# Causal masks of pass one written into PSUM by the scalar engine instead of by matmuls, the slots of both passes put side by side, and one sum moved to GpSimd

## The reference, cut to what matters

```python
x  = L0_attn_x                                   # (32, 256, 128): 32 images of 256 tokens
xn = layernorm(x)
# branch 1: rotary attention, 16 heads of width 8
scores = einsum(q_rot, k_rot) / sqrt(8) + decay_bias      # (b, 16, 256, 256)
scores = where(causal, scores, -inf)
attn_1 = softmax(scores) @ v ;  out_1 = attn_1 @ Wo.T
# branch 2: one head of width 128 whose q, k, v, o are mixtures over 8 experts,
# gated by rw = gating(layernorm(xn)); then a gated mixture of 8 experts as feed-forward
hs    = n + attn_out ;  out_2 = hs + moe(layernorm(hs))
return x + out_1 + out_2
```

## Time and profile before

| what | value |
|---|---|
| median of 3 runs | 1262.35 us (1260.88 to 1263.69) |
| the profiled execution, its own time | 1263.52 us |
| its span, first to last instruction | 1261.7 us |
| granted TensorE clock, mean (1 is full speed) | 0.985 |
| PE busy | 1177.7 us, 93% |
| DVE busy | 1030.4 us, 82% |
| ACT busy | 710.2 us, 56% |
| POOL busy | 220.9 us, 18% |
| start of the first mask product (L1498) of step 1, of step 30 | 98.58 us, 951.33 us |

### The profile page before, as it was taken

The page is one execution under the profiler, slowest core; times in us unless marked ns, Lnnn a source line. Parts: engine busy times, 40 slices in busy tenths (PEclk is TensorE's granted clock), DMA queues, the critical chain, the costliest instruction groups (busy, mean ns, idle before and its releaser), DMA issues.

```text
span 1261.7 us, 33146 instructions
## 1 busy us (share of the span) xinstructions
PE 1177.7 (93%) x10652; PEld 899.4 (71%) x10652; DVE 1030.4 (82%) x3704; ACT 710.2 (56%) x1286; POOL 220.9 (18%) x338
## 2 busy tenths in 40 slices
PE   2399999999999999999999999999999899999998
PEld 1167777777777777777777777777777677777776
DVE  8878888888888888888888888888876667777664
ACT  2155565665666666655666666666665744555532
POOL 4212222222222222222222222222223000000000
PEclk9789999999999999999999999999999999999999
DMA  3433332333333333323323333333331044444453
GB/s 97 131 109 91 89 91 85 89 100 95 111 85 91 88 88 87 90 87 95 85 85 88 96 107 101 88 87 91 90 85 55 10 157 169 169 170 179 188 188 132
DMA packets 103113, 133.01 MB, mean 105 GB/s; under 512 B 13576, under 2 KB 82424, under 8 KB 94864
## 3 DMA queue, kind: packets, MB, share of 16 engines
q1 hardware_dynamic: 100548, 130.72, 33.3%
q10 hardware_dynamic: 2508, 1.58, 0.4%
HBM read 109.12 MB, written 21.54 MB: 104 GB/s over the span
## 4 chain that ended last, share of the span: by engine, by line
PE 45%; DVE 29%; issue 15%; ACT 7%; DVEq 3%; DMA 1%; POOL 0%; ACTq 0%; SPq 0%; POOLq 0%
PE ps L1838 9%; PE ps L1824 9%; PE ps L1621 4%; DVE mx L1175 3%; PE ps L1448 3%; PE ps L1552 3%; ACT ps L759 3%; ACT pr L753 3%; PE ps L1575 2%; PE ps L1576 2%; DVE rots L1100 2%; PE ps L1611 2%; DVE rots L1091 2%; PE ps L1585 1%; DVE rots L1095 1%
## 5 line engine op out<-in xcount | busy, mean ns | idle before, releaser
L753 ACT ACTIVATE pr<-ps 128x1024 f32<-128x1024 f32 x192 | 196.7, 1025 | 109.4 <-PE ps L1535 76.2
L1175 DVE TENSOR_REDUCE mx<-ps 128x4 f32<-128x1024 f32 (+1 forms) x192 | 234.9, 1224 | 20.1 <-PE ps L1508 12.0
L621 POOL TENSOR_TENSOR n1s<-rep,n1T 128x256 f32<-128x256 f32 x256 | 177.0, 729 | 299.5 <-DVE mpart L1189 279.5
L759 ACT ACTIVATE ps<-trn 128x1024 f32<-128x1024 bf16 x191 | 196.4, 1028 | 4.1
L1838 PEld LDWEIGHTS ps<-w2s,ats 128*128 128x128 f32 x1024 | 131.7, 192 | 51.2 <-issue 46.8
L1575 PE MATMUL ps<-n1s,wqk 128*128 128x256 f32 x512 | 163.7, 402 | 0.0
L1576 PE MATMUL ps<-n1s,wqk 128*128 128x256 f32 x512 | 153.2, 381 | 0.0
L950 ACT ACTIVATE n1s<-ps 128x512 f32<-128x512 f32 x128 | 76.5, 597 | 123.1 <-PE ps L1824 121.9
L1585 PE MATMUL ps<-wv,n1s 128*128 128x128 f32 x1024 | 141.6, 281 | 0.0
L1838 PE MATMUL ps<-w2s,ats 128*128 128x128 f32 x1024 | 135.7, 276 | 1.9 <-DVE ats L1378 1.9
L1585 PEld LDWEIGHTS ps<-wv,n1s 128*128 128x128 f32 x1024 | 126.7, 191 | 11.5 <-issue 6.5
(11 more groups left out here) (230 smaller groups left out, 2041.0 us busy)
## 6 DMA issues: line engine op xcount, KB each, us to landing
rep<-scr_rw SPq DMA_DIRECT2D x32, 1024.0 KB, 5.7
stk<-scr_rw SPq DMA_DIRECT2D x16, 1024.0 KB, 8.0
scr_parts<-parts SPq DMA_DIRECT2D x64, 192.0 KB, 5.8
stk<-scr_parts SPq DMA_DIRECT2D x248, 48.0 KB
rots<-scr_rw SPq DMA_DIRECT2D x8, 1024.0 KB, 4.7
wqk<-scr_rw SPq DMA_DIRECT2D x8, 1024.0 KB, 9.3
stk<-scr_parts SPq DMA_DIRECT2D x248, 32.0 KB
xt<-in_x SPq DMA_DIRECT2D x32, 128.0 KB, 2.1
```

What stands on the lines that cost most here:

```text
L621: pool.tensor_tensor(n1s[:, e], rep[:, par, e], n1T[:, par], ALU.mult).then_inc(n1s_done, 1)
L753: act.activation(pr[:, Q, :, i], ps[:, S2[0]:S2[0] + NF], ACT.Exp).then_inc(exp_done, 1)
L759: act.activation(ps[:, S2[0]:S2[0] + NF], seeds[:, kind:kind + 1].broadcast_to((P, NF, 512)), ACT.Copy).then_inc(seed_done, 1)
L1175: dve.tensor_reduce(mx[:, min(i, 1)].rearrange("p (f h) -> p f h", f=NF)[:, :, h:h + n], ps[:, S1[0]:S1[0] + NF].rearrange("p f (h t) -> p ...
```

## The change

Four things are done.

1. `mask_l`, `mask_r`, `mask_half`, their eight DMAs, three VectorE instructions and all mask products of `unit1` are gone. A new tile `seeds1` (two kinds, bf16) is made in the prologue, and ScalarE's new `seed_max(b, k)` copies it over both banks of S1 before each unit of pass one. It waits until `row_max` of the unit before has read them; `unit1` waits for `seed1_done`.
2. ScalarE's and TensorE's orders are rearranged: on TensorE unit2(k) stands right behind unit1(k) everywhere, and qk 0 goes ahead of unit1(0); on ScalarE seed_max(n + 1, k + 1) stands right behind exps(n, k), and that of unit 0 at the end of the step before.
3. The sum `bs` moves from VectorE's add_hs to GpSimd's new `add_base`, the last thing in GpSimd's step.
4. In the prologue GpSimd's scale(0) no longer waits for max_parts(0). The transposes of norm_T and the products of proj set their start flag on the first one of a bank only; the banks of S1 are prepared by `plant_seeds` too.

```diff
+            def seed_max(b, k, front=None):
+                act.wait_ge(s1_read, UNITS * b + k)
+                if front is not None:
+                    act.wait_ge(rot_chain, ROT_LINKS * front + 2)
+                kind = 1 if k % 3 else 0
+                act.activation(ps[:, S1[0]:S1[0] + NF], seeds1[:, kind:kind + 1].broadcast_to((P, NF, 512)), ACT.Copy
+                               ).then_inc(seed1_done, 1)
...
 ScalarE, step:
                 exps(n, 0)
+                next_seed(1)
...
                 exps(n, 1)
+                next_seed(2)
...
                 exps(n, 2)
+                next_seed(3)
...
+                exps(n, 3)
                 evac_qk(n)
-                exp_slot(n, 3)
+                next_seed(4)
                 evac_pv(n, 0)
-                seed_slot(n, 3)
+                exps(n, 4)
+                next_seed(5)
...
                 soft_exp(n)
-                exps(n, 4)
...
                 if n_x:
                     put_max(n + 1, 1 - u)
+                if n_x >= 2:
+                    seed_max(n + 2, 0, n + 3 if n_x == 3 else None)
...
 ScalarE, prologue:
+            seed_max(0, 1)
             evac_weights(0)
             evac_logits(1)
             evac_v(1, 1)
+            for k in range(2, 4):
+                seed_max(0, k)
             upper_stacks(1, 1, 0, stack_in)
+            seed_max(0, 4)
+            seed_max(0, 5)
             gate_tanh(1)
             upper_stacks(1, 1, 1, stack_in)
...
             evac_norm_x(2, LATER)
+            seed_max(1, 0, 2)
...
 TensorE, unit1:
-                pe.wait_ge(s1_read, UNITS * b + k)
-                for f in range(NF):
-                    bank = ps[:, S1[f]]
-                    if i == 0:
-                        mm(bank, mask_l[ROWS[f]], mask_r[ROWS[f]].rearrange("p h t -> p (h t)"), start=True, stop=False,
-                           skip_group_check=True)
-                    else:
-                        mm(bank.rearrange("p (h t) -> p h t", h=2)[:, :, P:S], mask_l[ROWS[f]], mask_r[ROWS[f], 0:2],
-                           start=True, stop=False, skip_group_check=True)
+                pe.wait_ge(seed1_done, UNITS * b + k + 1)
...
 TensorE, step:
+                qk(n, 0)
                 next_max(0)
                 unit2(n, u, 0)
-                qk(n, 0)
                 qk(n, 1)
...
                 next_max(3)
+                unit2(n, u, 3)
                 qk(n, 7)
-                unit2(n, u, 3)
                 pv(n, u, 0)
...
                 next_max(4)
+                unit2(n, u, 4)
                 soft_scores(n)
                 ve(n, 0)
                 out_T(n, 0)
                 ve(n, 1)
                 ve(n, 2)
+                ve(n, 3)
                 next_max(5)
-                unit2(n, u, 4)
+                unit2(n, u, 5)
...
-                for e in range(3, 7):
+                for e in range(4, E):
                     ve(n, e)
-                unit2(n, u, 5)
-                ve(n, 7)
...
 GpSimd:
-                pool.wait_ge(max_chain, (MAX_LINKS + 1) * (b + 1))
+                if not isinstance(b, int) or b:
+                    pool.wait_ge(max_chain, (MAX_LINKS + 1) * (b + 1))
...
+            def add_base(n, u):
+                pool.wait_ge(hs_done, n + 1)
+                pool.wait_ge(xa_done, n + 1)
+                pool.wait_ge(base_stored, 16 * n)
+                hv = hs[:, T * n:T * n + T] if isinstance(n, int) else hs[:, bass.ds(n * T, T)]
+                pool.tensor_tensor(bs[:, u], hv, xa[:, u], ALU.add).then_inc(base_done, 1)
...
 VectorE, add_hs:
-                dve.wait_ge(hs_done, n + 1)
-                dve.wait_ge(xa_done, n + 1)
-                dve.wait_ge(base_stored, 16 * n)
-                dve.tensor_tensor(bs[:, u], hv, xa[:, u], ALU.add).then_inc(base_done, 1)
```

More of the change, by code:

```diff
@@ L49 @@
 STACK_DMAS = NF * (1 + SLOT_DMAS)
-NEAR, FAR, FAINT = 2.0 ** 41, 2.0 ** 126, 2.0 ** -85
 LN2_LINKS = 3 + 10
@@ L94 @@
 BIAS_LINKS = 9
-CASTS = 5
+CASTS = 8
 BF16_ONES = float(np.array([0x3F803F80], np.uint32).view(np.float32)[0])
@@ L146, in build @@
         mask_in = sb("mask_in", [P, 2, P])
-        mask_half = sb("mask_half", [P, 4, P])
         mask_qk = sb("mask_qk", [P, 2, P], BF16)
-        mask_l = sb("mask_l", [P, P], BF16)
-        mask_r = sb("mask_r", [P, HG, P], BF16)
+        seeds1 = sb("seeds1", [P, 2, 512], BF16)
         wa = sb("wa", [P, 5, D])
@@ L248, in build @@
         FIRST, LATER = (G0, PVB), (S1[0], S1[1])
-        ld_const, ld_w, ld_half, cb_stored = sem("ld_const"), sem("ld_w"), sem("ld_half"), sem("cb_stored")
+        ld_const, ld_w, cb_stored = sem("ld_const"), sem("ld_w"), sem("cb_stored")
         ld_ident, ld_theta, ld_sim, ld_wa, ld_w2, rows_in = (
             sem("ld_ident"), sem("ld_theta"), sem("ld_sim"), sem("ld_wa"), sem("ld_w2"), sem("rows_in"))
-        sim_chain, bias_chain, mask_made, cast_done = (
-            sem("sim_chain"), sem("bias_chain"), sem("mask_made"), sem("cast_done"))
+        sim_chain, bias_chain, cast_done = sem("sim_chain"), sem("bias_chain"), sem("cast_done")
         set_dve, set_act, set_pe, set_pool, set_dma = (
@@ L296, in build @@
         seed_done = sem("seed_done")
+        seed1_done = sem("seed1_done")
         exp_done = sem("exp_done")
@@ L638, in step @@
                     scale(n + 1, 1 - u)
+                add_base(n, u)
             second_norm(0)
@@ L685, in make_seeds @@
                 act.activation(seeds[:, 1].rearrange("p (h t) -> p h t", h=HG), mask_in[:, 1:2].broadcast_to((P, HG, P)),
+                               ACT.Copy).then_inc(cast_done, 1)
+                halves = seeds1[:, 1].rearrange("p (h a t) -> p h a t", h=2, a=2)
+                act.activation(halves[:, :, 0], ones_p[:].rearrange("p (o t) -> p o t", o=1).broadcast_to((P, 2, P)),
+                               ACT.Copy, scale=0.0).then_inc(cast_done, 1)
+                act.activation(halves[:, :, 1], mask_in[:, 0:1].broadcast_to((P, 2, P)), ACT.Copy).then_inc(cast_done, 1)
+                act.activation(seeds1[:, 0].rearrange("p (h t) -> p h t", h=HG), mask_in[:, 0:1].broadcast_to((P, HG, P)),
                                ACT.Copy).then_inc(cast_done, 1)
@@ L851, in step, with next_seed @@
                     evac_norm_1(n + 2, u)
+                def next_seed(k):
+                    if n_x:
+                        seed_max(n + 1, k)
                 exps(n, 0)
+                next_seed(1)
                 if n_x >= 2:
@@ L914, in _ @@
             upper_stacks(0, 0, 0, first_in)
+            act.wait_ge(set_pe, 2)
+            seed_max(0, 0)
             gate_tanh(0)
@@ L1067, in _ @@
             assert ch.k == SIN_READY, ch.k
[L1069 to L1075, removed]
             dve.wait_ge(set_act, 5)
@@ L1429, in plant_seeds @@
                 pe.wait_ge(cast_done, CASTS)
-                for j in range(2):
-                    mm(ps[:, S2[j]], identb[:], seeds[:, 0], start=True, stop=False, skip_group_check=True)
+                for bank in S1 + S2:
+                    ins = mm(ps[:, bank], identb[:], seeds[:, 0], start=True, stop=False, skip_group_check=True)
+                ins.then_inc(set_pe, 1)
             def norm_T(b, banks, free):
@@ L1439, in norm_T @@
                     for i in range(T):
-                        ins = pe.transpose(ps[:, banks[0], (T * k + i) * P:(T * k + i + 1) * P], src[:, i], ident[:])
+                        ins = mm(ps[:, banks[0], (T * k + i) * P:(T * k + i + 1) * P], src[:, i], ident[:],
+                                 start=(k == 0 and i == 0), stop=True, is_transpose=True, skip_group_check=True)
                 ins.then_inc(xzT_out, 1)
@@ L1447, in proj @@
                 for side in range(2):
-                    ins = mm(ps[:, banks[1], side * S:(side + 1) * S], wa[:, 2 * side], xnT[:], start=True, stop=True)
+                    ins = mm(ps[:, banks[1], side * S:(side + 1) * S], wa[:, 2 * side], xnT[:], start=(side == 0), stop=True,
+                             skip_group_check=True)
                 ins.then_inc(rot_out, 1)
@@ L1485, in unit1 @@
                     pe.wait_ge(xnT_done, front + 1)
-                    pe.wait_ge(rot_chain, ROT_LINKS * front + 2)
                 if i == 0:
@@ L1779, in _ @@
             proj_v(0, False)
+            pe.wait_ge(sim_chain, 2)
             plant_seeds()
@@ L1782, in _ @@
             pe.wait_ge(rows_in, 16 * N_ROWS)
-            pe.wait_ge(mask_made, 3)
             unit1(0, 0, 0)
```

## The result

The changed kernel takes 1379.26 us (median of 4 runs, 1378.12 to 1380.32) against 1262.41: the ratio is 1.0929, 95% interval [1.0914, 1.0943]. That is 117 us slower; forecast were 108, and a range of 1330 to 1412. The profiled execution took 1378.12 us with a span of 1376.3.

A forecast was written before the change was run, and what follows sets the result against it. TensorE's own work, 97% busy, was taken to bound the kernel. 102 us for the steps and 5 for the prologue add 107 to a span of 1261.7, making 1369; the forecast was 1370 us, range 1330 to 1412.

The forecast's parts named there:

- The ring: Pass one, ScalarE and TensorE: mask copy, units, exponential and pass-two copy wait on each other; one turn takes 3.76 us.
- The rival of a hidden ring: Pass one: the turn hides under TensorE's work; 1213 us at best, 1233 without the gap's removal; chance 0.04.
- The step walked through: One full step followed on TensorE, ScalarE and VectorE: 32.7 us against 29.4, 102 us in 31 steps.
- the late VectorE: End of a step: VectorE is free for normalise(1) 0.27 us late, and TensorE's att_T with it.
- The prologue: Before the steps: the first mask copies and ScalarE's later work run late, costing 5 us, bounds 0 and 8.
- The wait behind six DMA issues: Prologue, ScalarE: seed_max(0, 4) stands behind issues of 3.37 us, moving row_max(0, 4) from 49.20 to about 55.0.
- The sum: Whole kernel: 102 us for the steps and 5 for the prologue make 107 on a span of 1261.7.
- I cost it at nothing: VectorE in each step: taking its sum of 0.43 us away gains nothing, since VectorE waits for TensorE in every unit.
- its own case: Whole kernel: the forecast of 1370 us with its bounds, 1350 to 1395; chance 0.70.
- the case of VectorE in time: Lower bound of the step's loss: 3.0 us a step if VectorE is not late at the step's end.
- The clock rival: TensorE in the steps: short gaps also lower its clock, 31 to 62 us on top, 1400 to 1430; chance 0.15.
- the gap before unit2(5): TensorE's wait before the last unit of pass two, 0.8 us a step; said to go if the ring hides.

The follow-up runs named there:

- e3: e1 with the ScalarE mask copy of pass one writing only columns 0 to 255 of each bank: 1292.15 us.
- e4: e1 with ScalarE's mask copy for the next unit placed between the exponential and the pass-two copy, not behind both: 1311.53 us.
- e1: The changed kernel with 14 one-column memsets added to VectorE's prologue: 1354.96 us.
- e8: Kernel before with units and ScalarE work reordered, sum on GpSimd, 14 memsets and qk 0 ahead of unit 0; TensorE still writes the masks: 1228.96 us.
- e9: e8 with only unit 0's mask copied by ScalarE at the end of the step before, and GpSimd's scale(0) freed: 1225.82 us.
- e2: The kernel before with only the sum `bs` moved from VectorE to GpSimd: 1301.81 us.
- e5: e2 with the 14 memsets of e1 in VectorE's prologue: 1258.30 us.
- e6: The kernel before with unit2(3), (4), (5) right behind their unit1 on TensorE, and ScalarE's exps 3 and 4 before the evacuations: 1228.54 us.

## Why the prediction was right, and what it missed

**The ring: right, and shown.** The prediction said that the mask copy stands in a closed circle of exponential, copy, copy and two units, and that it is the turn and not ScalarE's busy share that sets the step. A turn was worked out at 3.76 and measured 3.74. E3 takes 0.43 us from one link and the turn loses 0.43; e4 rearranges the same links and the turn loses 0.36 to e1, 0.28 expected; e8 takes the copies out and the step loses 3.9 us. The rival of a hidden ring fell with the first gap.

**The step walked through: right to 0.3 us.** 32.7 forecast, 32.37 in a clean step and 32.36 on average in e1. What was too much is the late VectorE: 0.27 us for normalise(1). Row_max(5) starts 0.43 after the products of a small unit (656.05 to 656.48), not the 0.55 I took from a unit of kind 0, and the chain behind it was a little shorter, so VectorE was in time.

**The prologue: the number right, half of the way to it by luck.** 5 us forecast. The products of unit 0 of step 0 start at 72.18 us, against 66.64 plus 0.23 for the mask products: 5.3 later. The wait behind six DMA issues (3.30 us) is there, but costs less than worked out: row_max(0, 4) is at 53.38 (55.0 forecast, 49.20 before), and the xzT forecast at 67.0 starts at 64.71, 2.7 us late and not 5. The rest comes from a wait that the prediction did not have, as in e9: the copy of unit 0 of image 1 waits for VectorE's rotation, with rwT behind it. The first row is of the kernel before, the others of the changed one:

```profile
64.99 0.27 ACT L734 ACTIVATE rwT<-ps 16x128 f32<-16x128 f32 x1 [2.38 <-PE ps L1477]
...
68.91 1.03 ACT L779 ACTIVATE ps<-seeds 128x1024 f32<-128x1024 bf16 x1 [3.60 <-DVE rots L1117]
69.87 0.25 ACT L741 ACTIVATE rwT<-ps 16x128 f32<-16x128 f32 x1
70.17 1.22 PE L1590 MATMUL ps<-n1s,wqk 128*128 128x256 f32 x2 [2.52 <-ACT rwT L741]
```

**The sum: mis-sized by a term that was not in it.** 102 for the steps and 5 for the prologue make 107. In spans, e1 is 91.4 us over the kernel before (1353.1 less 1261.7): 5.6 by att_T of step 0, 87.1 from there to att_T of step 31, and 1.3 given back behind it. To this the changed kernel adds 24.3 for the fetches. So the forecast of 107 stood between 91 and 117 and was near the result because an oversized term (3.3 us a step; 2.9 measured) covered part of a missing one. What was missing is a step of its own: that instructions taken out of VectorE's stream cost time. "I cost it at nothing" was said of the sum on GpSimd; in e2 it costs 39 us with the fetches, and in e5 it gains 4 without them. The range held because its width was meant for other things. Two of the prediction's own sums slip a little, and nothing hangs on them: 93 us on 1262 make 1355, not 1350, for the low end of its own case, and 1262 - 29 + 5 is 1238, not 1233, in the rival of the hidden ring. That low end was the case of VectorE in time, which is what the traces show, and e1, the ring without the stops, measured 1354.96.

**The clock rival: a small part of it came true.** Across the clean steps the granted clock is 1.00 with five gaps of up to 1.2 us. Behind the gaps of 2.6 to 2.9 us of the stopped steps it fell in six cases of twelve (0.58 for 4 us at 611.54, as it did behind the 2.45 us of the earlier trace rows) and stayed at 1.00 in the others, so the length of the gap alone does not settle it. In the ring of the clean steps it fell nowhere. The Trainium skill's rule in "TensorE: Matmul & The Clock Gate", section "A second HAM failure mode: psum-queue depth-cycling", by which frequent short idling makes the clock swing, did not hold for this ring.

**What the rearrangement does.** The prediction named the gap before unit2(5) only in a rival. E6 shows that removing it is the better half of this change: 34 us, lost under a ring that costs 126.

## What to carry to other kernels

Before moving work to an engine with idle time, write down what stands before it in that engine's order and what waits behind it on the engine it came from. If the two meet, the sum of one turn decides and not the busy shares; a copy of 1.03 us cost next to nothing in the steps outside the ring (e9) and about 0.8 us of step for each of the five inside it (32.36 us a step in e1 against 28.25 in e9). And when a kernel with hardware loops changes by a few instructions, look at the instruction queues of the page and for "issue" stops at the loop's edge before explaining the time by the edit: here a pad of 14 instructions was worth 24 and 43 us.

## What the runs showed of the hardware that was not expected

A loop of VectorE with 347 instructions a turn in the trace (register and semaphore ones counted; 352 where the sum is still in it) ran with no fetch in its turns at one place of the stream and with about five at another, a few instructions earlier. Ahead of the loop the trace has 439 instructions of VectorE in the changed kernel and 442 in e2, and these two stop. It has 448 in the kernel before and e6, 452 in e1, e3 and e4, 455 in the rest, and none of these stops. Q14 had 26 packets (0.21 MB) in the kernel before, e1, and e3 to e9, and 85 (0.70 MB) in the changed kernel and e2: 59 more of 8.2 KB each in 12 backward jumps. VectorE then stops behind every jump, for 2.2 to 2.5 us at the loop's first row_max and for 1.0 to 1.6 us (in e2 1.3 to 2.0) at the statistics behind it. That q14 serves VectorE is inferred from the coincidence and from e1 and e5, where moving VectorE's stream alone ends both. The Trainium skill, "Runtime: NRT & Kernel Launch", section "Instruction fetch mechanics", says that a taken branch whose target has left the two pages that are held has to fetch it before execution goes on; the stops agree with it. The page's blocks are of 16 KiB; q14's packets are half of that, and no run shows whether two packets make a block. How far the loop may be moved on before it stops again was not tried.
